# The last two tiles of a transformer layer: copies in two parts, down products in banks of their own, and three normalises on another engine

## The reference

```
x = _layernorm(x + _L0_attn_ref(x, ...), axis=-1)
x = _layernorm(x + _L0_ffn_ref(x, ...), axis=-1)

def _L0_ffn_ref(x, w_gate, w_up, w_down):
    gate = fp4_linear(x, w_gate)
    y = fp4_linear(x, w_up)
    h = jax.nn.silu(gate) * y
    return fp4_linear(h, w_down)

fp4_linear: xq = fp4_quant_dequant(x); wq = fp4_quant_dequant(w); einsum('bsk,nk->bsn', xq, wq)
```

## Time and profile before

| | us |
|---|---|
| median of 3 runs | 695.15 |
| lowest, highest | 694.05, 695.99 |
| the profiled execution, its own time | 694.54 |
| its span, from the first to the last instruction | 692.5 |

### The profile page before, as it was taken

How to read it: one execution, slowest core, us unless ns; L and a number is a source line. 1 busy time by engine, 2 the same in 40 slices (tenths; PEclk the granted TensorE clock), 3 DMA queues, 4 the chain that set the end, 5 groups by cost and what they waited for, 6 DMA issues and landing times.

```text
span 692.5 us, 18033 instructions
## 1 busy us (share of the span) xinstructions
PE 677.2 (98%) x5586; PEld 644.8 (93%) x5586; DVE 631.5 (91%) x1501; ACT 571.9 (83%) x1353; POOL 573.8 (83%) x583
## 2 busy tenths in 40 slices
PE   8999999999999899999999999999999999999994
PEld 5899999999888799999999999999999999999994
DVE  5999999999999989998999898898999998999876
ACT  6899999987879978888777768776877998888886
POOL 5888888888888769998898889888878998888761
PEclk9999999999999999999999999999999999999998
DMA  5332323232331000000000000000000101111123
GB/s 159 100 92 74 98 74 92 86 92 79 92 89 59 18 1 1 2 1 1 1 2 1 2 1 1 2 1 1 2 1 2 46 32 47 44 35 41 60 69 122
DMA packets 40052, 29.86 MB, mean 43 GB/s; under 512 B 3731, under 2 KB 39958, under 8 KB 39958
## 3 DMA queue, kind: packets, MB, share of 16 engines
q1 hardware_dynamic: 37216, 26.49, 12.5%
q10 hardware_dynamic: 2742, 2.23, 1.2%
HBM read 20.32 MB, written 8.39 MB: 41 GB/s over the span
## 4 chain that ended last, share of the span: by engine, by line
PE 82%; POOL 5%; issue 5%; ACT 4%; DVE 3%; DMA 0%; ACTq 0%; POOLq 0%; DVEq 0%
PE bank L928 63%; PE wide L1071 6%; PE wide L928 5%; PE bank L1059 2%; PE bank L1010 2%; PE wide L1028 1%; PE bank L990 1%; POOL scratch L430 1%; POOL scratch L405 1%; PE bank L1091 1%; PE bank L1089 1%; POOL rounded L422 1%; ACT dump L525 1%; ACT res L530 1%; DVE rounded L883 0%
## 5 line engine op out<-in xcount | busy, mean ns | idle before, releaser
L928 PE MATMUL bank<-wf_hi,rounded 128*128 128x352 f32 (+1 forms) x1664 | 390.1, 312 | 0.8 <-DVE res L835 0.7
L928 PEld LDWEIGHTS bank<-wf_hi,rounded 128*128 128x128 f32 x1664 | 285.1, 189 | 1.5 <-issue 1.1
L928 PE MATMUL bank<-wf_lo,rounded 128*128 128x352 f32 (+1 forms) x832 | 256.2, 308 | 0.0
L928 PEld LDWEIGHTS bank<-wf_lo,rounded 128*128 128x128 f32 x832 | 157.5, 189 | 0.0
L928 PE MATMUL bank<-qkv_hi,rounded 128*128 128x512 f32 (+1 forms) x512 | 145.3, 350 | 0.9 <-ACT bank L498 0.7
L468 POOL TENSOR_TENSOR scratch<-scratch 128x704 bf16<-128x704 f32 x63 | 96.7, 1535 | 22.2 <-ACT scratch L649 19.9
L447 POOL TENSOR_TENSOR scratch<-scratch 128x704 f32<-128x704 bf16 x64 | 89.1, 1393 | 20.6 <-DVE scratch L876 20.6
L478 POOL TENSOR_TENSOR scratch<-scratch 128x704 f32<-128x704 f32 x64 | 94.3, 1474 | 14.3 <-DVE scratch L832 13.9
L928 PEld LDWEIGHTS bank<-qkv_hi,rounded 128*128 128x128 f32 x512 | 92.4, 192 | 14.3 <-ACT bank L502 2.0
L430 POOL TENSOR_TENSOR scratch<-scratch 128x512 f32<-128x512 f32 x64 | 68.0, 1063 | 24.2 <-DVE scratch L811 24.1
L928 PE MATMUL bank<-qkv_lo,rounded 128*128 128x512 f32 (+1 forms) x256 | 87.5, 342 | 0.0
(11 more groups left out here) (124 smaller groups left out, 1552.3 us busy)
## 6 DMA issues: line engine op xcount, KB each, us to landing
scratch<-x_feat SPq DMA_DIRECT2D x64, 128.0 KB, 2.2
scratch<-x_tok SPq DMA_DIRECT2D x64, 128.0 KB, 2.3
out<-scratch SPq DMA_DIRECT2D x48, 128.0 KB, 1.7
out<-res SPq DMA_DIRECT2D x16, 128.0 KB, 1.8
scratch<-w_ffn ACTq DMA_DIRECT2D x15, 128.0 KB, 2.1
scratch<-L_attn_Wq SPq DMA_DIRECT2D x1, 256.0 KB, 3.1
scratch<-L_attn_Wk SPq DMA_DIRECT2D x1, 256.0 KB, 3.3
scratch<-L_attn_Wv SPq DMA_DIRECT2D x1, 256.0 KB, 4.0
```

The source lines that it names most:

```text
L928: op = pe.matmul(dst, x(c), w(c), start=first and n == 0, stop=last and n == len(terms) - 1, skip_group_check=not first)
```

## The change

- `eps` and `ln_root` are declared behind `rounded`, the last of the large buffers, so all weights and working buffers move to lower addresses. Nothing else about them changes.
- `h_parts`: tile 62 goes in two parts too. `h_count(n)` counts the parts of the tiles before `n`, for the waits.
- `pd`: tile 62's down product goes to bank 4 and tile 63's to bank 2. Neither waits for `y_s` any more.
- Tiles 50, 51 and 52 are normalised by VectorE in step 67, right behind the residual add of tile 61 (`DVE_MID`). Before, 50 was VectorE's in step 66, and 51 to 53 were ScalarE's in step 67.
- ScalarE has only tile 54 in step 67, so the squares of tiles 62 and 63 stand in front of 53 and 55. VectorE normalises 56 to 59 all in step 69, behind the residual add of tile 63.
- The LayerNorm steps of tiles 56 to 59 start in step 67, not 66.
- `STORES` follows the new order; `BY_DVE` names VectorE's tiles for SyncE.

```diff
+BY_DVE = (50, 51, 52, 56, 57, 58, 59, 62, 63)
-ACT_OUT = {65: (48,), 66: (49,), 67: (51, 52, 53), 68: (54,), 69: (55,), 72: (60, 61)}
-DVE_OUT = {66: (50,), 68: (56, 57), 69: (58, 59), 72: (62, 63)}
-STORES = (48, 49, 50, 51, 52, 53, 56, 57, 54, 58, 59, 55, 62, 60, 63, 61)
-LN_B = ((0, 32, 2, 38), (32, 16, 2, 54), (48, 8, 4, 62), (56, 4, 7, 66), (60, 4, 7, 70))
+ACT_OUT = {65: (48,), 66: (49,), 67: (54,), 69: (53, 55), 72: (60, 61)}
+DVE_MID = {67: (50, 51, 52)}
+DVE_OUT = {69: (56, 57, 58, 59), 72: (62, 63)}
+STORES = (48, 49, 50, 51, 52, 54, 56, 57, 58, 53, 59, 55, 62, 60, 63, 61)
+LN_B = ((0, 32, 2, 38), (32, 16, 2, 54), (48, 8, 4, 62), (56, 4, 7, 67), (60, 4, 7, 70))
...
         silu_at = sb("silu_at", [P, 1])
-        eps = sb("eps", [P, 1])
-        ln_root = sb("ln_root", [P, T])
...
         taken_r = [0]
+        eps = sb("eps", [P, 1])
+        ln_root = sb("ln_root", [P, T])
...
-        pd = [bank[5]] * (NT - 1) + [bank[4]]
+        pd = [bank[5]] * (NT - 2) + [bank[4], bank[2]]
...
-            return [slice(0, 4), slice(4, IC)] if n == NT - 1 else [slice(0, IC)]
+            return [slice(0, 4), slice(4, IC)] if n >= NT - 2 else [slice(0, IC)]
+        def h_count(n):
+            return sum(len(h_parts(k)) for k in range(n))
...
-                if any(m in tiles for tiles in DVE_OUT.values()):
+                if m in BY_DVE:
...
-                        need(act, h_t, n + 1 + k)
+                        need(act, h_t, h_count(n) + 1 + k)
...
-                    need(act, h_lo, n + len(h_parts(n)))
+                    need(act, h_lo, h_count(n + 1))
...
+            def norms_out(tiles):
+                for n in tiles:
+                    need(dve, y_ln, ln_done(n))
+                    dve.tensor_scalar(res[:, rows(n)], res[:, rows(n)], rstd[:, n:n + 1], nbias[:, n:n + 1],
+                                      ALU.mult, ALU.add).then_inc(y_od, 1)
...
                                              accum_out=row_sum[:, NT + n:NT + n + 1]).then_inc(y_s, 1)
+                norms_out(DVE_MID.get(m, ()))
                 ln(6, m - 1)
...
-                        need(dve, h_hi, n + 1 + k)
+                        need(dve, h_hi, h_count(n) + 1 + k)
...
-                for n in DVE_OUT.get(m, ()):
-                    need(dve, y_ln, ln_done(n))
-                    dve.tensor_scalar(res[:, rows(n)], res[:, rows(n)], rstd[:, n:n + 1], nbias[:, n:n + 1],
-                                      ALU.mult, ALU.add).then_inc(y_od, 1)
+                norms_out(DVE_OUT.get(m, ()))
...
-                    need(pe, h_lo, n + 1)
-                    if n < NT - 1:
+                    need(pe, h_lo, h_count(n) + 1)
+                    if n < NT - 2:
...
-                        need(pe, h_lo, n + 2)
+                        need(pe, h_lo, h_count(n) + 2)
```

## The result

The changed kernel takes 689.38 us, median of 4 runs (689.09 to 690.76), against 695.12 us (694.05 to 695.99) for the kernel before: a ratio of 0.9922, 95% interval 0.9903 to 0.9941. So it is faster by 5.7 us by the medians and by 5.4 by the ratio, give or take 1.3.

A forecast was written before the change was run, and what follows sets the result against it. With TensorE busy 98% of the span, only the drain could win, bounded by SyncE's store queue: 694.54 - 0.77 = 693.77 us for the profiled execution, 0.61 below the median, so 694.4 us; range 692.9 to 695.8.

The forecast's parts named there:

- Parts 1 to 5: Drain: step times for the reordered last tiles; residual add of tile 63 1.00 us earlier, last LayerNorm at 685.95.
- the store queue: End of the drain: ten stores issued by SyncE 0.483 us apart decide the end, the last starting at 689.43, against 690.20.
- The drain's total: From the last gate-and-up product to the program's end: 0.77 us gained, limited by the stores.
- the stretch from 250 to 676 us unchanged: Sign of a right forecast: the long stretch before the drain, where TensorE is busy 424.51 of 426 us, stays the same.
- Part 6: Moving eps and ln_root shifts weights and scratch by some 64 bytes: no effect taken, bounds 2.8 us either way.
- (d): Rival on TensorE's matmuls: the shifted addresses save time, 691.6 us or below; chance 0.05.
- Rival (a): Drain: stores pile up behind tile 63's residual add if it stays at 685.29; 0.2 us slower, 695.4 us; chance 0.08.
- Rival (b): Drain: store issues spread nearer to 0.33 us, the last normalise decides; up to 1.8 us gained, 693.3 us; chance 0.12.
- The 2.04 us around the span: Outside the traced span: the profiled execution of before took 694.54 us, 2.04 of it around the span.
- part 3: VectorE's normalises of tiles 50 to 52 mid-drain: 0.33 us each, ending at 680.61, 0.07 us to spare.
- the rule of the Trainium skill: VectorE normalises in the drain: two elements per cycle, near 0.2 us each, for a sum of about -0.9 instead of -0.8.

The follow-up runs named there:

- e2: The changed kernel with eps and ln_root put back ahead of the weights, leaving only the edits of the last two tiles; 693.78 us, ratio 0.9982.
- f4: The changed kernel with padding that moves only scratch and rounded, so rounded stands 96 bytes beyond the weights (modulo 256); 690.25 us, one run.
- e1: The kernel before with only eps and ln_root moved behind rounded; 690.58 us, ratio 0.9939.
- k1: The changed kernel with eps and ln_root between wf_lo and scratch, so rounded stands 64 bytes beyond the weights (modulo 256); 684.43 us, ratio 0.9862.
- f3: The changed kernel with padding ahead of the weights and of scratch, so rounded stands 32 bytes beyond the weights (modulo 256); 689.28 us, one run.
- e4: The kernel before with 448 bytes of padding between wf_lo and scratch, so rounded stands 192 bytes beyond the weights (modulo 256); 690.20 us, one run.

## Why the prediction was right, and where it was wrong

Parts 1 to 5 and the store queue stand, each to 0.1 us (the table of the drain), and not by luck: each time is an interval between rows of before, with the next obstacle looked for. The drain's total was short by 0.07 us of 0.84. e2 alone measures 0.4 to 2.1 us gained, which holds 0.77. The sign "the stretch from 250 to 676 us unchanged" failed, and the last gate-and-up product ended 2.8 us earlier; the prediction had said what that would mean: the buffers.

Part 6 is the step that failed. It took nothing, between bounds of 2.8 us either way, for the moved buffers. Three faults lie in it. The neighbours were wrong: the earlier trace rows is one VectorE operation at two addresses, are DMAs; neither shows TensorE reading two operands at once, which is what the shift touched in 49 matmuls of every tile. The bound was of the wrong shape: 0.5 ns on each of 5586 matmuls, where it was 7.3 ns on each of 12 matmuls a tile (54 x 12 x 7.3 ns = 4.7 us, of which the down product took back 54 x 7 ns = 0.4) and nearly nothing on the rest. The nearest rows were those of L928 itself: one kind of matmul at 158 ns in five tiles and 166 in 57 shows that TensorE's rate isn't fixed, and by how much, and gives a bound: 57 x 12 x 7.3 ns = 5.0 us to win, and 5 x 12 x 7.3 ns = 0.4 to lose, as before was in the worse of the two nearly always. (No run shows a matmul that moves by 0.5 ns throughout, the term that the bounds rest on.) And the chances: "nothing speaks for either" is no reason for 0.05 each, and none for a range that leaves both out. With 5.0 us as the bound the range would have reached down to 689.4. That (d) stands in the list with the right sign is luck: no row was given for it.

Rival (a) did not occur, as the residual add of tile 63 came 0.99 us earlier. Rival (b), the queue at 0.33 us per issue, did not either; the pace was 0.477. That the queue of SyncE decides was right only in part: with a second issuer the drain shortened by only 0.25 us, with the DMA engines nearly as tight. The 2.04 us around the span nearly stayed (690.76 - 688.8 = 1.96). In part 3, four normalises took 1.38 us, 0.325 each with the last one's 0.08, as the row of before had it. So the rule of the Trainium skill ("VectorE: DVE Perf Modes", section "Mode 2×_2P"), two elements per cycle, isn't borne out after either.

Open are: what picks the rhythm when a stream starts, and why it differs between executions and perhaps chips; what let the clock fall in one execution; why the distance counts modulo 256; f4's 118.7 ns; and how much of the difference between e1 and the kernel before is an address and how much the odds of a history.

## What to carry to other kernels

Moving a buffer isn't free of cost or gain: whoever shifts the operands of a matmul stream that bounds the kernel may change the time of each of its matmuls, and should bound that by how much the same matmul already differs within the trace. Where TensorE is 98% busy, look at the distance between starts of equal matmuls, stretch by stretch; a page's mean hides 158 beside 166. Test several pads between moving and stationary operands: here 64 bytes were worth some 5 us of 690 (k1 against after), more than the whole reordered drain (0.84 us), while 32, 96 and 192 bytes (f3, f4, e4) brought nothing: 689.3 to 690.3 us.

## What the runs showed of the hardware

Every figure here is from the runs above. The time from one float32r matmul to the next depends on the distance of moving and stationary operand modulo 256 bytes: 113.4 to 120.0 ns for 256 columns, 158.3 to 160.0 for 352, and not on the absolute place (0 and 64 tried). At distance 128, a second rhythm of 166 to 167 ns can hold for a whole stretch of 352 columns, at identical addresses and with all other engines at rest, and differs between repeats; at distance 64, the 256 columns ran at 113.3 ns in one execution and at 117.5 in another. The granted clock was 0.50 for 3.4 us in the middle of one execution, behind 5 us in which TensorE was busy for 3.40; in another kernel's execution with the same 3.40 it stayed at 1.00. A store of 128 KB took 542 to 747 ns to issue from GpSimd, against 332 to 456 on SyncE; beside each other, the last stores of both landed 2.3 to 2.8 us after their issue began (SyncE's alone 1.7 to 1.9), and two issuers brought the landings from 0.489 to 0.463 us apart.
